# Slot attention: read weights made and read by 64-column tiles instead of 128-column ones

## Chip, cores and metric

One core of one Trainium2 chip runs the whole program. The metric is the device time of one execution in microseconds (us). The kernel before takes 5117.4 us, the median of 3 runs (5113.7 to 5121.28). All data is float32.

## What is computed

The program is a decoder of two layers over 4096 tokens (64 sequences of 64 tokens, 256 wide). The change touches only the first operation of the first layer, a gated slot attention with 16 heads, 128 slots per head and 128-wide keys and values. For each head and token it runs

```
gt = exp(g_t);  bw = beta_t * w_t
Sk = Sk * gt[None, :] + k_t[:, None] * bw[None, :]      # keys x slots
Sv = Sv * gt[:, None] + bw[:, None] * v_t[None, :]      # slots x values
a  = softmax(q_t @ Sk * SCALE)                          # over the slots
o_t = a @ Sv
```

and then normalizes `o_t`, gates it with a sigmoid, projects it with Wo and adds it to X. The recurrence restarts with each sequence of 64 tokens.

## The kernel before

The function `gsa` has no step-by-step scan. A token t reads what an earlier token s has written, weighed by the product of the gates between them. That product is built by levels: at level b (1, 2, 4, 8, 16, 32) it links a block of b tokens with its partner block of b tokens. So the read weights (source s by reader t) are a diagonal (s = t) and six levels, each of which is right only inside its own blocks.

The work is cut in pairs: `pair(h, gp)` runs 4 times for each head h, 64 times in all, and a pair has two halves, named a and b by the ends of the tile names, with 4 tiles of 128 tokens each (a tile is two sequences). The halves are the same code half a pair apart, on PSUM banks 0 to 3 (a) and 4 to 7 (b). In one call of `pair` three generations are in flight: `within` (new, n), `before` (m = n - 1) and `earlier` (l = n - 2). Each engine has its own list of these steps, written out by hand, and the lists meet only at semaphores. Each engine runs its list strictly in order, so a wait holds all that stands behind it.

Names of half a (half b is alike, its lines are in brackets):

- `GWVa` holds the gates (columns 0 to 511), the write weights w (512 to 1023) and the values v. The levels of decay are multiplied into w in place (`early`, `late`).
- `Pa` (six levels of packed left factors) and `AMa` (six levels of packed right factors) feed the level matmuls. DVE makes `AMa` in six products from `AAa`, the softmax weights, and the gates (L1527 to L1540, signal `reach_a_by_dve`).
- PE makes each level with two 128x128 matmuls (L1222, L1230, L1238, L1243, L1247, L1254; signal `weights_a_by_pe`), interleaved with other PE work and before the projection L1260.
- The diagonal is the row sum of `WTa * CAa` (four tensor_tensor_reduce on DVE, L1517), which POOL spreads over `QKa[:, 512:1024]` (L1895).
- DVE lays the levels over it with six predicated copies (L1534, L1539, L1544, L1549, L1553, L1559; signal `weights_a_by_dve`), each between other DVE work.
- PE reads: four 128x128 matmuls of the values with these weights (L1265, signal `read_a_by_pe`), before the projection L1269.
- ACT waits for that read before it writes new write weights and values over `GWVa` (L1779, `Silu`, and L1784), squares the result for the norm (L1782), and evicts the next projection to `CWV` (L1791). DVE runs the convolution on that (L1588, L1602, L1617).
- PE's projection L1260 writes PSUM bank 6. Until then bank 6 holds the output gate, which ACT evicts in L1765 (`SGb`, signal `sigmoid_b_by_act`). PE waits for that before L1260.
- A half begins for ACT with the exponentials of its softmax (L1740 for a, L1656 for b), which wait for the scaled maximum of DVE (L1499, L1365).

The wait of ACT, unchanged by the diff:

```python
if before:
    act.wait_ge(read_a_by_pe, m * 2 + 1)
nc.scalar.activation(forward(GWVa[:, 512:1536]), forward(CWV[:, :]), ACT.Silu).then_inc(silu_a_by_act, 1)
```

Of the kernel before, what the change touches and what calls it, by code (L numbers as in the profile page):

```python
# [6 lines left out]
I32 = mybir.dt.int32  # L7
# [771 lines left out]
def gsa(nc, io, X, PS, IDENT, FLIP, shared, blank):  # L779
    ctx = ExitStack()  # L780
    with ctx:
# [16 lines left out]
        MASKS = sb("masks", [128, 7, 256])  # L798
# [5 lines left out]
        GWVa, GWVb = sb("gwva", [128, 1536]), sb("gwvb", [128, 1536])  # L804
# [7 lines left out]
        Pa, Pb = sb("pa", [128, 6, 256]), sb("pb", [128, 6, 256])  # L812
# [8 lines left out]
        dcola, dcolb = sb("dcola", [128, 4]), sb("dcolb", [128, 4])  # L821
# [200 lines left out]
        with nc.Block() as block:  # L1022

            @block.tensor
            def _(pe):
                pe.wait_ge(setup_by_pool, 1)
                pe.wait_ge(setup_loads_sp, 48)

                def pair(h, gp, within=True, before=True, earlier=True, eldest=True):
# [5 lines left out]
                    if before:  # L1035
                        if earlier:
                            pe.wait_ge(residual_a_by_dve, l * 1 + 1)
                        for e in range(2):
                            last = nc.tensor.transpose(tile(PS[3][:, 0:256], e), tile(Pa[:, 1, :], e), IDENT[:, :])
# [10 lines left out]
                    if before:  # L1050
                        pe.wait_ge(turned_a_by_act, m * 6 + 2)
                        for j in range(4):
                            last = nc.tensor.transpose(tile(PS[3], j), tile(GWVa[:, 1024:1536], j), IDENT[:, :])
# [8 lines left out]
                    if earlier:  # L1062
                        pe.wait_ge(reach_b_by_dve, l * 6 + 1)
                        for e in range(2):
                            last = nc.tensor.matmul(tile(PS[6][:, 0:256], e), tile(Pb[:, 0, :], e), tile(AMb[:, 0, :], e), start=True, stop=True)
                        last.then_inc(weights_b_by_pe, 1)
# [5 lines left out]
                    if earlier:  # L1072
                        pe.wait_ge(reach_b_by_dve, l * 6 + 3)
                        for e in range(2):
                            last = nc.tensor.matmul(tile(PS[4][:, 0:256], e), tile(Pb[:, 1, :], e), tile(AMb[:, 1, :], e), start=True, stop=True)
                        last.then_inc(weights_b_by_pe, 1)
                    if before:
                        pe.wait_ge(values_a_by_act, m * 1 + 1)
                        for e in range(2):
                            last = nc.tensor.transpose(tile(PS[3][:, 0:256], e), tile(Pa[:, 3, :], e), IDENT[:, :])  # L1080
                        last.then_inc(turned_a_by_pe, 1)
                    if earlier:
                        pe.wait_ge(weights_b_by_dve, l * 6 + 1)
                        for e in range(2):
                            last = nc.tensor.matmul(tile(PS[6][:, 0:256], e), tile(Pb[:, 2, :], e), tile(AMb[:, 2, :], e), start=True, stop=True)
                        last.then_inc(weights_b_by_pe, 1)
                        if before:
                            pe.wait_ge(sigmoid_b_by_act, m * 2 + 1)
                        for e in range(2):
                            last = nc.tensor.matmul(tile(PS[7][:, 0:256], e), tile(Pb[:, 4, :], e), tile(AMb[:, 4, :], e), start=True, stop=True)  # L1090
                        last.then_inc(weights_b_by_pe, 1)
                        pe.wait_ge(weights_b_by_dve, l * 6 + 2)
                        for e in range(2):
                            last = nc.tensor.matmul(tile(PS[4][:, 0:256], e), tile(Pb[:, 3, :], e), tile(AMb[:, 3, :], e), start=True, stop=True)
                        last.then_inc(weights_b_by_pe, 1)
# [3355 lines left out]
```

## Time and profile before

| | |
|---|---|
| median of 3 runs | 5117.4 us |
| profiled execution | 5121.28 us among the runs; its span 5121.6 us |
| PE busy | 4927.6 us, 96% of the span |
| DVE busy | 4230.1 us, 83% |
| ACT busy | 3733.4 us, 73% |
| POOL busy | 2307.0 us, 45% |

### The profile page before, as it was taken

How to read it: one execution, taken by the hardware profiler on the slowest of the kernel's cores; microseconds unless marked ns; L12 is line 12 of the kernel's file. 1: busy time of each engine (PE TensorE's matmuls, PEld its weight loads, DVE VectorE, ACT ScalarE, POOL GpSimd, SP SyncE). 2: the span in 40 equal slices, each digit the busy share in tenths (PEclk: the TensorE clock that was granted, in tenths of full speed). 3: DMA queues.
4: the chain of work that ended last, by engine and by line, in shares of the span. 5: the costliest groups of instructions: out<-in, count | busy, mean ns of one | idle time of the engine just before them, and what ended most of it. 6: DMA issues, size and time to landing. Idle time of an engine off the chain costs nothing. (4 is left out here: it accounts for less than half of the span.)

```text
span 5121.6 us, 113480 instructions
## 1 busy us (share of the span) xinstructions
PE 4927.6 (96%) x37926; PEld 3636.5 (71%) x37926; DVE 4230.1 (83%) x10048; ACT 3733.4 (73%) x9700; POOL 2307.0 (45%) x2976
## 2 busy tenths in 40 slices
PE   7999999999999999999999997979999989989899
PEld 4777777777777777777777776868756667778666
DVE  4999999999999999999999995869722378868423
ACT  4999999999999999999999995748713444446233
POOL 2555555555556565655555553741133200011332
PEclk9999999999999999999999998989999999999999
DMA  5500000000000000000000001010012471010225
GB/s 170 173 3 8 6 3 8 7 2 8 7 3 7 7 4 6 8 6 3 8 6 3 8 1 33 17 35 2 24 73 90 135 248 61 2 47 22 87 96 164
DMA packets 178268, 204.34 MB, mean 40 GB/s; under 512 B 28683, under 2 KB 165772, under 8 KB 177040
## 3 DMA queue, kind: packets, MB, share of 16 engines
q1 hardware_dynamic: 161840, 159.07, 10.2%
q0 software_dynamic: 12960, 34.63, 1.8%
q8 instruction: 332, 5.44, 0.4%
q10 hardware_dynamic: 2880, 3.10, 0.2%
q14 instruction: 256, 2.10, 0.1%
HBM read 157.95 MB, written 114.16 MB: 53 GB/s over the span
## 5 line engine op out<-in xcount | busy, mean ns | idle before, releaser
L471 ACT ACTIVATE sl<-PSA 128x512 f32<-128x512 f32 x58 | 34.6, 597 | 253.6 <-PE PSA L172 249.0
L1900 POOL TENSOR_TENSOR gsa_qkb<-gsa_qkb,gsa_tmpb 128x256 f32<-128x256 f32 x64 | 47.7, 745 | 316.3 <-DVE gsa_tmpb L1555 316.3
L1863 POOL TENSOR_TENSOR gsa_qka<-gsa_qka,gsa_tmpa 128x256 f32<-128x256 f32 x64 | 47.6, 744 | 312.1 <-DVE gsa_tmpa L1422 312.1
L274 DVE TENSOR_TENSOR hidden<-sl,PSA 128x512 f32<-128x512 f32 x60 | 41.2, 686 | 173.9 <-ACT sl L471 164.8
L1857 POOL TENSOR_TENSOR gsa_qkb<-IDENT,gsa_dcolb 128x512 f32<-128x512 f32 x64 | 66.5, 1039 | 187.4 <-DVE gsa_dcolb L1379 187.4
L1895 POOL TENSOR_TENSOR gsa_qka<-IDENT,gsa_dcola 128x512 f32<-128x512 f32 x64 | 66.5, 1040 | 184.3 <-DVE gsa_dcola L1517 184.3
L1111 PE MATMUL PSA<-XT,gsa_wa 128*128 128x512 f32 x256 | 123.2, 604 | 9.8 <-DMA gsa_wa<-in_w_heads 7.9
L415 DVE COPY ffn0b_hT<-PSA 128x256 f32<-128x256 f32 x71 | 30.2, 425 | 122.8 <-PE PSA L213 121.1
L415 DVE COPY ffn1b_hT<-PSA 128x256 f32<-128x256 f32 x71 | 30.1, 425 | 121.3 <-PE PSA L213 119.6
L548 POOL DMA_INDIRECT results<-ffn1b_Y,ffn1b_XI x71 | 69.8, 983 | 119.6 <-ACT ffn1b_Y L494 115.6
L548 POOL DMA_INDIRECT results<-ffn0b_Y,ffn0b_XI x71 | 69.5, 979 | 118.6 <-ACT ffn0b_Y L494 113.0
L1157 PE MATMUL PSA<-gsa_wo,gsa_sgb 128*128 128x256 f32 x512 | 122.7, 383 | 0.0
L1323 PE MATMUL PSA<-XT,gsa_wa 128*128 128x512 f32 x256 | 121.7, 598 | 0.0
L1122 PE MATMUL PSA<-XT,gsa_wa 128*128 128x512 f32 x256 | 121.6, 598 | 0.0
L3005 POOL TENSOR_TENSOR ffn0a_rstd<-ffn0a_mse,ffn0a_exponent 128x1 f32<-128x1 f32 x32 | 17.6, 551 | 230.7 <-DVE ffn0a_mse L2814 230.7
L1305 PE MATMUL PSA<-gsa_wo,gsa_sga 128*128 128x256 f32 x512 | 121.1, 379 | 0.0
L1178 PE MATMUL PSA<-XT,gsa_wa 128*128 128x512 f32 x256 | 121.0, 595 | 0.0
L1260 PE MATMUL PSA<-XT,gsa_wa 128*128 128x512 f32 x256 | 120.5, 593 | 0.0
L1191 PE MATMUL PSA<-XT,gsa_wa 128*128 128x512 f32 x256 | 120.5, 593 | 0.0
L1334 PE MATMUL PSA<-XT,gsa_wa 128*128 128x512 f32 x256 | 120.5, 593 | 0.0
L1269 PE MATMUL PSA<-XT,gsa_wa 128*128 128x512 f32 x256 | 120.4, 593 | 0.0
L2415 POOL TENSOR_TENSOR mlstm_rs<-mlstm_wide,mlstm_neghalf 128x16 f32<-128x16 f32 x32 | 96.0, 3000 | 45.1 <-DVE mlstm_wide L2277 44.9
(853 smaller groups left out, 19369.6 us busy)
## 6 DMA issues: line engine op xcount, KB each, us to landing
pairs<-in_blank SPq DMA_DIRECT2D x2, 35904.0 KB, 128.9
ffn0b_XS<-pairs SPq DMA_DIRECT2D x71, 132.0 KB
ffn1b_XS<-pairs SPq DMA_DIRECT2D x71, 132.0 KB
gsa_wa<-in_w_heads SPq DMA_DIRECT2D x64, 128.0 KB, 2.1
X<-in_x SPq DMA_DIRECT2D x8, 512.0 KB, 8.0
mlstm_CX<-in_ctx SPq DMA_DIRECT2D x32, 128.0 KB, 2.1
ffn0b_WGU<-results SPq DMA_DIRECT2D x8, 512.0 KB, 5.2
ffn0b_WD<-results SPq DMA_DIRECT2D x8, 512.0 KB, 6.0
```

The costliest lines, as they stand in the source:

```text
L548: nc.gpsimd.indirect_dma_start(RESULTS[:, :], bass.IndirectOffsetOnAxis(ap=XI[t % IS][:, :], axis=0), Y[t % YS][:, :], None, bounds_check= ...
L1111: last = nc.tensor.matmul(PS[2][:, :], WA[:, 3, c, :], XT[:, c, gp * 1024 + 0:gp * 1024 + 0 + 512], start=(c == 0), stop=(c == 1))
L1122: last = nc.tensor.matmul(PS[3][:, :], WA[:, 2, c, :], XT[:, c, gp * 1024 + 0:gp * 1024 + 0 + 512], start=(c == 0), stop=(c == 1))
L1157: last = nc.tensor.matmul(PS[6 + j // 2][:, (j % 2) * 256:(j % 2) * 256 + 256], tile(SGb[:, :], j), WO[:, :], start=True, stop=True)
L1178: last = nc.tensor.matmul(PS[0][:, :], WA[:, 1, c, :], XT[:, c, gp * 1024 + 0:gp * 1024 + 0 + 512], start=(c == 0), stop=(c == 1))
L1191: last = nc.tensor.matmul(PS[1][:, :], WA[:, 0, c, :], XT[:, c, gp * 1024 + 0:gp * 1024 + 0 + 512], start=(c == 0), stop=(c == 1))
L1260: last = nc.tensor.matmul(PS[6][:, :], WA[:, 3, c, :], XT[:, c, gp * 1024 + 512:gp * 1024 + 512 + 512], start=(c == 0), stop=(c == 1))
L1269: last = nc.tensor.matmul(PS[7][:, :], WA[:, 2, c, :], XT[:, c, gp * 1024 + 512:gp * 1024 + 512 + 512], start=(c == 0), stop=(c == 1))
L1305: last = nc.tensor.matmul(PS[2 + j // 2][:, (j % 2) * 256:(j % 2) * 256 + 256], tile(SGa[:, :], j), WO[:, :], start=True, stop=True)
L1323: last = nc.tensor.matmul(PS[4][:, :], WA[:, 1, c, :], XT[:, c, gp * 1024 + 512:gp * 1024 + 512 + 512], start=(c == 0), stop=(c == 1))
L1334: last = nc.tensor.matmul(PS[5][:, :], WA[:, 0, c, :], XT[:, c, gp * 1024 + 512:gp * 1024 + 512 + 512], start=(c == 0), stop=(c == 1))
L2415: nc.gpsimd.tensor_tensor(rs[b][:, :], wide[b][:, :], NEGHALF[:, :], ALU.pow).then_inc(rs_by_pool, 1)
```

## The change

`GWVa` grows to 2048 columns, so that the raw write weights survive beside the decayed ones. The read weights of a tile are kept as 64 columns for each of its two sequences: sequence r lies on partitions 64r to 64r + 63. All levels, and the diagonal too (raw write weights times `AAa`), come from matmuls with 64 stationary columns (a column tile) and 64 or 32 moving columns, in one burst. DVE then multiplies the diagonal by a mask and lays six levels over it, one behind the other. The read is eight matmuls on 64 rows each (row tiles) and its result lies in two banks. The sums on DVE and the spreading on POOL for the diagonal go. A new mask array of 512 KB is loaded at the start of `gsa`; the old one shrinks from 896 to 768 KB.

On PE, for half a (b is alike, on banks 4, 6 and 6, 7). The six levels of two matmuls each, L1222 to L1254, stood before the projection L1260, with waits for DVE between them. The burst stands right behind L1260, and the read behind L1269, L1275 and L1279 (a projection and slots of half b), right ahead of the transposes L1285:

```diff
-  pe.wait_ge(reach_a_by_dve, m * 6 + 1)
-  for e in range(2):
-      last = nc.tensor.matmul(tile(PS[2][:, 0:256], e), tile(Pa[:, 0, :], e), tile(AMa[:, 0, :], e), ...)
-  last.then_inc(weights_a_by_pe, 1)
...
   if within:
       if before:
           pe.wait_ge(sigmoid_b_by_act, m * 2 + 2)
       for c in range(2):
           last = nc.tensor.matmul(PS[6][:, :], WA[:, 3, c, :], XT[:, c, ...], ...)
   if before:
-      pe.wait_ge(weights_a_by_dve, m * 6 + 6)
-      for j in range(4):
-          last = nc.tensor.matmul(tile(PS[2], j), tile(GWVa[:, 1024:1536], j), tile(QKa[:, 512:1024], j), ...)
-      last.then_inc(read_a_by_pe, 1)
+      pe.wait_ge(reach_a_by_dve, m * 6 + 6)
+      for j in range(4):
+          for r in range(2):
+              nc.tensor.matmul(PS[0][64*r:64*r+64, j*64:j*64+64], part(GWVa[:, 1024:1536], 2*j+r), part(flat(AAa), 2*j+r), ...)
+      for j in range(4):
+          for r in range(2):
+              nc.tensor.matmul(PS[2][64*r:64*r+64, j*32:j*32+32], part(GWVa[:, 1024:1536], 2*j+r), step_rights(AMa[:, 0, :], j, r), ...)
+      for k, bank, at0 in ((1, 0, 256), (2, 2, 128), (3, 0, 384), (4, 2, 256), (5, 2, 384)):
+          for e in range(2):
+              for r in range(2):
+                  last = nc.tensor.matmul(PS[bank][64*r:64*r+64, at0+e*64:at0+e*64+64], part(Pa[:, k-1, :], 2*e+r), part(AMa[:, k, :], 2*e+r), ...)
+      last.then_inc(weights_a_by_pe, 1)
...
+  if before:
+      pe.wait_ge(weights_a_by_dve, m * 7 + 7)
+      if within:
+          pe.wait_ge(sigmoid_a_by_act, n * 2 + 1)
+      for j in range(4):
+          for r in range(2):
+              last = nc.tensor.matmul(PS[2 + r][:, j*64:j*64+64], tile(GWVa[:, 1536:2048], j)[64*r:64*r+64, :], part(QKa[64*r:64*r+64, 512:768], j), ...)
+      last.then_inc(read_a_by_pe, 1)
```

On DVE, for half a. The six products of `AMa` stay, now without copies between them. The six copies of 128x256 (L1534, L1539, L1544, L1549, L1553, L1559) become a product and six copies of 128x128, behind L1564, L1568 and L1569 and ahead of L1572 and L1575. Those for 4, 8, 16 and 32 look like the one for 2 and wait each for the one before:

```diff
-  for j in range(4):
-      last = nc.vector.tensor_tensor_reduce(tile(WTa[:, :], j), tile(CAa[:, :], j), ..., dcola[:, j:j + 1])
-  last.then_inc(diagonal_a_by_dve, 1)
...
-  nc.vector.copy_predicated(rights(QKa[:, 512:1024], 4), packs(MASKS[:, 2, :].bitcast(I32), 4), packs(PS[2][:, 0:256], 4)).then_inc(weights_a_by_dve, 1)
...
+  dve.wait_ge(weights_a_by_pe, m + 1)
+  nc.vector.tensor_tensor(QKa[:, 512:768], PS[0][:, 0:256], WMASKS[:, 0:256], ALU.mult).then_inc(weights_a_by_dve, 1)
+  dve.wait_ge(weights_a_by_dve, m * 7 + 1)
+  dve.sem_inc(passed_by_dve, 1)
+  nc.vector.copy_predicated(square_step_rights(QKa[:, 512:768]), WMASKS[:, 256:384]..., PS[2][:, 0:128]...).then_inc(weights_a_by_dve, 1)
+  dve.wait_ge(weights_a_by_dve, m * 7 + 2)
+  dve.sem_inc(passed_by_dve, 1)
+  nc.vector.copy_predicated(square_rights(QKa[:, 512:768], 2), packs(level_mask(1), 2), packs(PS[0][:, 256:384], 2)).then_inc(weights_a_by_dve, 1)
...
-  nc.vector.scalar_tensor_tensor(SGa[:, :], SGa[:, :], NW[:, 0:1], PS[2][:, :], ALU.mult, ALU.mult)
+  for r in range(2):
+      last = nc.vector.scalar_tensor_tensor(of_part(SGa[:, :], r), of_part(SGa[:, :], r), NW[:, 0:1], PS[2 + r][:, 0:256]..., ALU.mult, ALU.mult)
```

On ACT, the copy of the step-1 left factors (L1793) becomes one of the odd raw write weights into the decayed ones, of the same size, and the square L1782 reads two banks. On POOL, L1895 goes, and the product of the softmax sums (L1901) waits for `softmax_a_by_act`. On SP:

```diff
   nc.sync.dma_start(MASKS[:, :, :], io["masks"]).then_inc(setup_loads_sp, 16)
+  nc.sync.dma_start(WMASKS[:, :], io["weight_masks"]).then_inc(setup_loads_sp, 16)
```

## Rows read from the trace of the kernel before

**Rows 1.** The page, part 1: busy us (share of the span) xinstructions.

```profile
PE 4927.6 (96%) x37926; PEld 3636.5 (71%) x37926; DVE 4230.1 (83%) x10048; ACT 3733.4 (73%) x9700; POOL 2307.0 (45%) x2976
```

**Rows 2.** Busy time by stretch: stretch, length, busy us of PE, PEld, DVE, ACT, POOL, clock.

```profile
1000.00:1500.00 500.00, 497.67 (x2786) 362.14 (x2785) 497.44 (x1176) 459.90 (x1223) 293.40 (x388) 1.00 0.02 5
...
3098.00:3109.00 11.00, 7.49 (x29) 5.46 (x29) 3.53 (x9) 1.09 (x2) 1.02 (x1) 0.83 0.00 0
```

**Rows 3.** Timeline of ACT in one half: start us, length us, engine, line, what, [idle before].

```profile
1010.52 0.37 ACT L1740 ACTIVATE gsa_caa<-PSA,gsa_nmxa 128x128 f32<-128x128 f32 x1 [0.31 <-DVE gsa_nmxa L1499]
...
1017.52 0.68 ACT L1765 ACTIVATE gsa_sgb<-PSA,gsa_bg 128x512 f32<-128x512 f32 x1
...
1019.51 0.42 ACT L1772 ACTIVATE gsa_pb<-gsa_gwvb 128x256 f32<-128x256 f32 x1 [0.73 <-DVE gsa_gwvb L1550]
...
1020.52 1.28 ACT L1779 ACT_TABLE_LOAD   x1
1021.86 0.63 ACT L1779 ACTIVATE gsa_gwva<-gsa_cwv 128x512 f32<-128x512 f32 x1
...
1023.70 1.10 ACT L1791 ACTIVATE gsa_cwv<-PSA,gsa_wcv 128x1024 f32<-128x1024 f32 x1
...
1033.81 0.37 ACT L1656 ACTIVATE gsa_cab<-PSA,gsa_nmxb 128x128 f32<-128x128 f32 x1 [0.30 <-DVE gsa_nmxb L1365]
```

**Rows 4.** Timeline of PE in the same half.

```profile
1014.96 0.61 PE L1222 MATMUL PSA<-gsa_ama,gsa_pa 128*128 128x128 f32 x4
...
1017.94 0.61 PE L1247 MATMUL PSA<-gsa_ama,gsa_pa 128*128 128x128 f32 x4
1018.38 0.38 PE L1250 MATMUL PSA<-IDENT,gsa_pb 128*128 128x128 f32 x2
...
1019.05 1.88 PE L1260 MATMUL PSA<-XT,gsa_wa 128*128 128x512 f32 x4
1020.77 1.05 PE L1265 MATMUL PSA<-gsa_qka,gsa_gwva 128*128 128x128 f32 x8
1021.66 1.88 PE L1269 MATMUL PSA<-XT,gsa_wa 128*128 128x512 f32 x4
```

**Rows 5.** Timeline of DVE in the same half.

```profile
1018.72 0.45 DVE L1549 COPY_PREDICATED gsa_qka<-gsa_masks,PSA 128x256 f32<-128x256 int32 x1
...
1020.06 0.43 DVE L1559 COPY_PREDICATED gsa_qka<-gsa_masks,PSA 128x256 f32<-128x256 int32 x1
...
1025.21 1.26 DVE L1588 SCALAR_TENSOR_TENSOR gsa_cwv<-PSA,gsa_wcv,gsa_cwv 128x1008 f32<-128x1008 f32 x1
...
1033.11 0.66 DVE L1365 TENSOR_SCALAR gsa_nmxb<-gsa_mxb 128x4 f32<-128x4 f32 x1
```

**Rows 6.** Groups of instructions from 1000 to 1500 us: busy us, mean ns, idle.

```profile
L1517 DVE CUSTOM_DVE_ANT_0 gsa_wta<-gsa_caa,gsa_wta 128x128 f32<-128x128 f32 x44 | 10.0, 279 | 0.0
...
L1534 DVE COPY_PREDICATED gsa_qka<-gsa_masks,PSA 128x256 f32<-128x256 int32 x11 | 7.9, 721 | 0.0
...
L1539 DVE COPY_PREDICATED gsa_qka<-gsa_masks,PSA 128x256 f32<-128x256 int32 x11 | 7.9, 714 | 0.0
...
L1544 DVE COPY_PREDICATED gsa_qka<-gsa_masks,PSA 128x256 f32<-128x256 int32 x11 | 4.7, 430 | 0.0
...
L1555 DVE TENSOR_TENSOR gsa_tmpb<-PSA,gsa_gb 128x256 f32<-128x256 f32 x11 | 4.6, 418 | 0.0
```

**Rows 7.** Timeline of PE where it switches to tiles of the array, later stages.

```profile
3210.84 0.38 PE L2131 MATMUL PSA<-IDENT,mlstm_CX 128*128 128x128 f32 x2
3211.15 2.04 PE L2188 MATMUL PSA<-mlstm_V,mlstm_S 64*64 64x17 f32 x64
...
3417.03 1.13 PE L2630 MATMUL PSA<-ffn0a_V,ffn0a_PT 128*64 128x34 f32 x32
3417.98 1.07 PE L2669 MATMUL PSA<-ffn0a_WV,ffn0a_xT 128*64 128x128 f32 x16
```

**Rows 8.** DMA issues from 64 to 75 us: count, KB, median us to landing.

```profile
gsa_masks<-in_masks SPq DMA_DIRECT2D x1, 896.0 KB, 4.8
```

More of the change, by code:

```diff
@@ L1219, in pair @@
                     if before:
-                        pe.wait_ge(reach_a_by_dve, m * 6 + 1)
-                        for e in range(2):
-                            last = nc.tensor.matmul(tile(PS[2][:, 0:256], e), tile(Pa[:, 0, :], e), tile(AMa[:, 0, :], e), start=True, stop=True)
-                        last.then_inc(weights_a_by_pe, 1)
                         pe.wait_ge(level_b_by_dve, m * 6 + 1)
@@ L1244, in pair @@
[L1244 to L1250 removed]
+                            last = nc.tensor.transpose(tile(PS[5][:, 0:256], e), tile(Pb[:, 1, :], e), IDENT[:, :])
@@ L1251, in pair @@
                         last.then_inc(turned_b_by_pe, 1)
-                        pe.wait_ge(weights_a_by_dve, m * 6 + 3)
-                        for e in range(2):
-                            last = nc.tensor.matmul(tile(PS[2][:, 0:256], e), tile(Pa[:, 5, :], e), tile(AMa[:, 5, :], e), start=True, stop=True)
-                        last.then_inc(weights_a_by_pe, 1)
                     if within:
@@ L1280, in pair @@
                         last.then_inc(slots_b_by_pe, 1)
+                    if before:
+                        pe.wait_ge(weights_a_by_dve, m * 7 + 7)
+                        if within:
+                            pe.wait_ge(sigmoid_a_by_act, n * 2 + 1)
+                        for j in range(4):
+                            for r in range(2):
+                                last = nc.tensor.matmul(PS[2 + r][:, j * 64:j * 64 + 64], tile(GWVa[:, 1536:2048], j)[64 * r:64 * r + 64, :], part(QKa[64 * r:64 * r + 64, 512:768], j), start=True, stop=True)
+                        last.then_inc(read_a_by_pe, 1)
                     if within:
@@ L1671, in pair @@
                         for j in range(4):
[L1672 removed]
+                            last = nc.scalar.activation(tile(GWVa[:, 1536:2048], j), tile(PS[3], j), ACT.Copy, scale=c4a[:, j:j + 1])
                         last.then_inc(values_a_by_act, 1)
@@ L4324, in level_masks @@
     out = []
-    for lv in range(6):
+    for lv in range(1, 6):
         b = 2 ** lv
@@ L4331, in level_masks, with weight_masks @@
     return np.stack(out, 1)
+def weight_masks():
+    s, t = np.arange(128)[:, None] % 64, np.arange(64)[None, :]
+    out = [np.tile(s == t, (1, 4))]
+    u = np.arange(32)[None, :]
+    out += [s == 2 * u, s == 2 * u, s == 2 * u + 1, s == 2 * u + 1]
+    for lv in range(1, 6):
+        block = t // 2 ** lv
+        partner = np.where(block % 2 == 1, block - 1, block + 1)
+        out.append(np.tile(s // 2 ** lv == partner, (1, 2)))
+    return np.concatenate(out, 1).astype(np.float32)
 def mirrored(x):
```

320 lines of the change are left out of this document (138 added, 182 removed).

## Prediction, written before the change was run

> **What bounds the kernel now.** I read the page first: PE 96%, DVE 83%, ACT 73% busy [rows 1]. Then the busy time by stretch, because the change lives in the slot attention alone (74 to 3070 us of 5121.6). From 1000 to 1500 us PE is busy 497.7, DVE 497.4 and ACT 459.9 of 500 us [rows 2]: three engines are nearly full, at a granted clock of 1.00. The reader should see that no engine has more than 8% to give, so a wait of some microseconds that hits one of them isn't hidden; it comes out at the end. A pair takes 46.7 us, a half 23.3: ACT starts the softmax of half a at 1010.52 and that of half b at 1033.81 [rows 3]. There are 64 pairs, so 128 halves.
>
> Next I laid the three queues of one half beside each other. ACT goes without a hole from L1740 to the eviction of the output gate, L1765, which ends at 1017.52 + 0.68 = 1018.20. It idles 0.73 us at L1772 and 0.30 us before L1656 [rows 3]. Its wait for the read (L1779) costs nothing today: the read L1265 ends at 1020.77 + 1.05 = 1021.82, and the table load for L1779 ends at 1021.80 [rows 3, 4]. PE starts L1260 at 1019.05 [rows 4], 0.85 us after the gate that it must wait for was evicted, so that wait costs nothing either. These two waits are the ones to watch.
>
> **The change, part by part.** I follow half a; half b has the same order of steps on every engine.
>
> (1) Level matmuls. Removed: 12 matmuls, 24 records. The four of one level take 1018.38 - 1017.94 = 0.44 us from the start to the next start [rows 4] (0.61 is the length with the modelled end, which overlaps the next), so 2.66 us. Added: 8 + 8 + 20 = 36 matmuls, 72 records, on 64 stationary columns. Tiles that lie side by side run at once: 32 records with 34 moving columns take 3417.98 - 3417.03 = 0.95 us, 0.029 each; with 128 moving columns 16 records take 1.07 us, of which the last alone is 0.27, so 0.054 each [rows 7]. Ours move 64 or 32 columns. I take 0.029 (for a pair 0.058, and half of the 0.109 for 128 columns is 0.055): 72 x 0.029 = 2.09 us. The upper bound is 72 x 0.054 = 3.9 us. Switching PE to tiles costs about 0.1 us: two transposes from 3210.84 would be through at 3211.06, the tiles start at 3211.15 [rows 7]. PE itself gains some 0.5 us by the levels and loses 0.4 by four switches. So PE's own work hardly changes.
>
> (2) Where the burst stands. Before, the levels filled PE from 1014.96 on [rows 4], while ACT worked towards L1765. Now they stand behind L1260, and L1260 waits for L1765. Ahead of it remain L1226, L1234 and L1250, eight records of 0.11 us with nothing late to wait for, so PE is through at about 1015.9 and then idles some 2.4 us. That is an added wait; queued behind it are L1260, the burst, L1269, L1275, L1279 and the read. So L1260 starts at 1018.20 + 0.15 = 1018.35, lasts 1.72 to the next start [rows 4], then 0.1 + 2.09: the burst's last start is over at 1022.26 and its last record lands at about 1022.43. The six products of DVE that it needs are ready at about 1017 and don't matter.
>
> (3) The evacuation. DVE's copies were spread among other work; now a product and six copies stand in a row, each waiting for the one before. Product of 128x256 from PSUM: 0.42 us by L1555. Copies of 128x256 take 430 ns at block 4 and 721 and 714 ns at blocks 1 and 2 [rows 6]. Those of 128x128 aren't in the trace; the slope between the two forms isn't either. Halving the elements and keeping some 0.16 us fixed gives 0.30 for four of them and 0.44 for the first two (bounds 0.22 to 0.43, and 0.30 to 0.72). The gap between dependent ones: a copy that waited for PE started 1018.72, when the matmuls L1247 had ended at 1018.55 [rows 4, 5], 0.17 us later; dependent DVE instructions without a wait instruction of their own show some 0.03. I take 0.13, near the first, since each copy here has such a wait. Sum: 0.42 + 2 x 0.44 + 4 x 0.30 + 6 x 0.13 = 3.28 us (2.4 to 3.9). It starts about 1022.48 and ends about 1025.76. PE meanwhile does L1269 (1.72) and L1275, L1279 (0.89) and is through at 1024.9.
>
> The Trainium skill, "TensorEngine Tiling (Array Packing)", section Performance Considerations (PSUM Bottleneck), says that tiling speeds up TensorE but not the evacuation of PSUM. That speaks against this change, and the rows above agree with it: 2.09 us on PE are followed by 3.28 us on DVE. Were the evacuation sped up like the matmuls, the sum below would be some 200 us smaller.
>
> (4) The read. L1559 ended at 1020.49 and L1265 started at 1020.77 [rows 4, 5], a lag of 0.28. So the read starts at 1026.04. Its 16 records have 128 stationary columns on 64 rows. No row shows that form with both row tiles in use. If the two run at once, as the 64x64 tiles do (64 records in 2.04 us [rows 7]), they last as long as the eight of L1265, 1.05 us; if not, 1.9. I take 1.05: the read ends at 1027.09 and ACT starts L1779 at 1027.13.
>
> (5) What it sets. L1779 started at 1021.86 [rows 3]: 5.27 us later. ACT had finished its table load at about 1021, since the wait at L1772 (0.73) is gone, so it now stands idle some 6 us in each half. Behind it on ACT are L1782, L1784, L1791 and all to the next softmax; the 0.30 us before L1656 are slack, so 4.97 remain. By DVE it is nearly the same: L1791 ends 2.94 after L1779 begins, at 1030.07; L1588 needs it and moves from 1025.21 to 1030.10, and from there DVE had no hole up to L1365, whose end at 1033.77 [rows 5] becomes 1038.66. Two chains end within 0.1 us of each other, so neither alone could be shortened for a gain. Half: 23.3 + 4.96 = 28.25 us.
>
> (6) What is saved elsewhere is hidden behind this. Four reductions (279 ns each [rows 6]), POOL's spreading, and some 0.6 us of copies come off engines that now wait; the split of L1579 adds about 0.12 us on DVE beside ACT. I count these at nothing: they lie between L1740 and the burst, where the burst waits for ACT. ACT's changed copies have equal sizes: nothing.
>
> (7) Start. SP loads 512 KB more and 128 KB less before the first weights; 896 KB landed in 4.8 us [rows 8]. In proportion 384 KB cost about 2 us once (0 to 5), as all engines wait for it.
>
> **Sum.** 5121.6 + 128 x 4.96 + 2 = 5758 us for the profiled execution, which stands 4 us (0.1%) above the median. So 5754, and I say 5755.
>
> **The rivals.**
> Faster. The place is DVE: if ACT and PE could run the chain of (2) to (4) beside other work, DVE's full queue would be the bound, and it loses per half about 0.85 us of reductions and 0.6 of copies, and gains 0.12: 1.3 us, 128 x 1.3 = 170, giving 4950 us. For it speaks that DVE is at 497.4 of 500 [rows 2]. Against it: ACT would have to be able to start L1779 no later than today, while the chain behind L1765 is 0.15 + 1.72 + 0.1 + 2.09 + 3.28 + 1.05 and lags, 8.9 us, and ACT has 2.8 us of work to put beside it. It decides as soon as that chain is shorter than about 3.7 us. 5%.
> Tiles that don't overlap. If the burst goes at 0.054 and the read's row tiles take turns, +1.8 and +0.85 per half: 5755 + 128 x 2.65 = 6095 us. Against it: both forms of tile ran in pairs in later stages [rows 7]. 7%.
> The clock falls. PE would have holes of 2.4, 1.1 and 1.6 us in each half. Where it was busy 7.5 of 11 us the granted clock was 0.83, here 1.00 [rows 2]. At 0.83 the 4.9 us of PE on the chain (1.72 + 2.19 + 1.05) become 5.9: 5755 + 128 x 1.0 = 5885 us. Wholly at the lower of the clock's two levels, 1.2 instead of 2.4 GHz, they would double: 6380. 12%, mostly near 5885. The Trainium skill, "TensorE: Matmul & The Clock Gate", Part 1, says that the throttled state is the default and activity lifts it, which points the same way; whether these holes suffice no row here shows.
> Partly absorbed. Copies and gaps at their lower bounds (2.4 instead of 3.28) and 0.2 less in the lags: +3.9 per half, 5620 us. 8%.
> That it doesn't do what it says (copies of half the size that cost as much as before): +0.13 x 4 + 0.28 x 2 = 1.1 us in each half: 5895 us. 6%.
>
> **How the numbers follow.** The forecast, 5755 us, has 62%, its own range 5660 to 5850. The range that should hold 8 in 10 takes in the absorbed case, the copies and the mild clock case: 5600 to 5990. It leaves out the faster case, the tiles in turn and the deep clock case. About 0.2% is what a measurement of this kernel can tell from no change. All cases but the first rival are slower by far more than that: slower 0.94, within it 0.01, faster 0.05.
>
> **What would show it.** In the profile after: a half of about 28 us; ACT idle about 6 us before L1779's counterpart (and L1691's), released by the read on PE; PE idle about 2.4 us before the projection of L1260, released by ACT's output gate; DVE's seven instructions in a row over 3.3 us; the level burst in 2.1 us with two records per 0.058 us. ACT's busy share from 1000 to 1500 us, 92% now [rows 2], should be near 76%. If ACT shows no wait for the read, or DVE's copies are short and overlap, I am wrong. If PE's clock is below 1.00 in the slot attention, the clock rival holds.

## The result and the profile after

The changed kernel takes 6054.87 us (median of 4 runs, 6047.3 to 6068.79), the kernel before beside it 5118.67 us (5113.7 to 5121.28): 936 us more, a ratio of 1.184 with a 95% interval of 1.183 to 1.186. The profiled execution has a span of 6045.5 us against 5121.6. The forecast was 5755 (+637), its range ended at 5990.

The page of the kernel after, part 1, answers to [rows 1]:

```profile
PE 5254.6 (87%) x45094; PEld 3839.7 (64%) x45094; DVE 4208.9 (70%) x9280; ACT 3713.3 (61%) x9700; POOL 2194.6 (36%) x2848
```

No engine is nearly full any more. Busy time by stretch of the kernel after (stretch, length, busy us of PE, PEld, DVE, ACT, POOL, granted clock), with the stretch of [rows 2] first and four pieces of single halves behind it:

```profile
1000.00:1500.00 500.00, 420.78 (x3015) 302.80 (x3016) 376.76 (x801) 348.24 (x933) 207.90 (x276) 0.89 0.02 5
1050.40:1052.90 2.50, 0.29 (x3) 0.05 (x1) 1.90 (x6) 2.40 (x6) 0.53 (x1) 1.00 0.04 13
1052.90:1060.00 7.10, 7.04 (x88) 4.58 (x88) 4.06 (x9) 2.73 (x5) 3.21 (x6) 1.00 0.01 2
1022.10:1025.60 3.50, 3.46 (x4) 1.18 (x4) 2.03 (x3) 2.72 (x5) 3.20 (x6) 0.54 0.02 5
1036.60:1039.50 2.90, 2.90 (x10) 2.38 (x9) 2.90 (x8) 2.90 (x11) 2.22 (x4) 0.59 0.00 0
```

The clock is 0.89 where it was 1.00 [rows 2], and it isn't spread evenly: near 1.00 in most pieces, and at 0.5, its lower level of 1.2 GHz, in stretches of some 3 to 7 us, each of which begins in one of PE's holes or within 1.3 us behind it (one goes from 1062.85 to 1069.68, behind the three holes of the half below).

The timeline of PE in one half a (start us, length us, engine, line, what, [idle before]) answers to [rows 4]. L1248 is the projection L1260 of before, L1254 to L1261 are the burst, L1283 is the read:

```profile
1050.31 0.38 PE L1242 MATMUL PSA<-IDENT,gsa_pb 128*128 128x128 f32 x2
1052.94 1.98 PE L1248 MATMUL PSA<-XT,gsa_wa 128*128 128x512 f32 x4 [2.25 <-ACT gsa_sgb L1751]
1054.86 0.69 PE L1254 MATMUL PSA<-gsa_aaa,gsa_gwva 128*64 128x64 f32 x16
1055.37 0.61 PE L1257 MATMUL PSA<-gsa_ama,gsa_gwva 128*64 128x32 f32 x16
1055.81 1.36 PE L1261 MATMUL PSA<-gsa_ama,gsa_pa 128*64 128x64 f32 x40
1057.10 1.98 PE L1265 MATMUL PSA<-XT,gsa_wa 128*128 128x512 f32 x4
...
1060.75 1.11 PE L1283 MATMUL PSA<-gsa_qka,gsa_gwva 64*128 64x64 f32 x16 [0.77 <-DVE gsa_qka L1554]
1063.58 1.12 PE L1289 MATMUL PSA<-IDENT,gsa_gwva 128*128 128x128 f32 x4 [1.73 <-ACT gsa_gwva L1770]
```

The same half on DVE, against [rows 5]: the product and the six copies, with 0.15 us between one's end and the next one's start.

```profile
1057.22 0.42 DVE L1536 TENSOR_TENSOR gsa_qka<-PSA,gsa_wmasks 128x256 f32<-128x256 f32 x1 [1.70 <-PE PSA L1261]
1057.80 0.44 DVE L1539 COPY_PREDICATED gsa_qka<-gsa_wmasks,PSA 128x128 f32<-128x128 int32 x1
...
1058.97 0.30 DVE L1545 COPY_PREDICATED gsa_qka<-gsa_wmasks,PSA 128x128 f32<-128x128 int32 x1 [0.15 <-DVE gsa_qka L1542]
...
1060.31 0.30 DVE L1554 COPY_PREDICATED gsa_qka<-gsa_wmasks,PSA 128x128 f32<-128x128 int32 x1
```

And on ACT, against [rows 3]. The wait that cost nothing before is now 6.25 us:

```profile
1045.21 0.37 ACT L1726 ACTIVATE gsa_caa<-PSA,gsa_nmxa 128x128 f32<-128x128 f32 x1
...
1052.20 0.68 ACT L1751 ACTIVATE gsa_sgb<-PSA,gsa_bg 128x512 f32<-128x512 f32 x1
...
1061.90 0.63 ACT L1765 ACTIVATE gsa_gwva<-gsa_cwv 128x512 f32<-128x512 f32 x1 [6.25 <-PE PSA L1283]
```

From here on a half has two parts: the head, from ACT's first exponential to its Silu, and the tail, from the Silu to the first exponential of the next half. Both are read from ACT's timeline. Means over the pairs between about 500 and 2900 us, in us:

| kernel | head a | tail a | head b | tail b | pair | time less that of before, same chip |
|---|---|---|---|---|---|---|
| before | 11.34 | 11.97 | 11.34 | 12.11 | 46.76 | 0 |
| forecast | 16.61 | 11.64 | 16.61 | 11.64 | 56.50 | +637 |
| after | 17.06 | 13.52 | 17.91 | 12.94 | 61.43 | +936 |

The forecast's head is 1027.13 - 1010.52. In the half shown above it is 1061.90 - 1045.21 = 16.69: there the chain is as forecast, and nothing in it ran at half clock. In others it is up to 18.6. The pattern of heads (16.7, 18.2, 18.6) and tails (12.6, 13.7, 13.9) repeats every four pairs. Where the 299 us beyond the forecast (936 - 637) are stands in the groups of PE's instructions between 1000 and 2000 us (busy us, mean ns of one, idle before). L1309 and L1170 are the output projections of the two halves, L1107 and L1248 the projections behind the output gate, L1126 and L1191 two others of the same form:

```profile
L1309 PE MATMUL PSA<-gsa_wo,gsa_sga 128*128 128x256 f32 x136 | 54.2, 571 | 0.0
L1107 PE MATMUL PSA<-XT,gsa_wa 128*128 128x512 f32 x64 | 50.9, 943 | 36.2 <-ACT gsa_sga L1668 36.2
L1170 PE MATMUL PSA<-gsa_wo,gsa_sgb 128*128 128x256 f32 x128 | 49.0, 553 | 0.0
L1248 PE MATMUL PSA<-XT,gsa_wa 128*128 128x512 f32 x64 | 38.3, 728 | 36.0 <-ACT gsa_sgb L1751 36.0
...
L1126 PE MATMUL PSA<-XT,gsa_wa 128*128 128x512 f32 x64 | 31.7, 618 | 0.0
L1191 PE MATMUL PSA<-XT,gsa_wa 128*128 128x512 f32 x64 | 30.1, 593 | 0.0
```

Projections elsewhere run at the length of before. Of the projections only the two that follow a hole, and the output projections that follow the holes around the read, are slow; so are the small transposes between the read and the output projection (L1299: 438 ns, where e1_filled below has 290).

### The profile page after: what moved, and what is told of

It is laid out like the page before. It is cut to its first block and busy times, and to the rows that moved or that the text cites. A ratio compares the mean times of both kernels' runs of the same rounds, so it can differ in the third digit from the quotient of the medians.

```text
span 6045.5 us, 127114 instructions
## 1 busy us (share of the span) xinstructions
PE 5254.6 (87%) x45094; PEld 3839.7 (64%) x45094; DVE 4208.9 (70%) x9280; ACT 3713.3 (61%) x9700; POOL 2194.6 (36%) x2848
## 3 DMA queue, kind: packets, MB, share of 16 engines
q14 instruction: 255, 2.09, 0.1%
## 5 line engine op out<-in xcount | busy, mean ns | idle before, releaser
L1107 PE MATMUL PSA<-XT,gsa_wa 128*128 128x512 f32 x256 | 204.5, 946 | 150.8 <-ACT gsa_sga L1668 142.1
L1248 PE MATMUL PSA<-XT,gsa_wa 128*128 128x512 f32 x256 | 156.1, 741 | 141.6 <-ACT gsa_sgb L1751 141.6
L1856 POOL TENSOR_TENSOR gsa_qka<-gsa_qka,gsa_tmpa 128x256 f32<-128x256 f32 x64 | 46.5, 727 | 598.4 <-DVE gsa_tmpa L1440 598.4
L1890 POOL TENSOR_TENSOR gsa_qkb<-gsa_qkb,gsa_tmpb 128x256 f32<-128x256 f32 x64 | 46.6, 727 | 552.0 <-DVE gsa_tmpb L1568 552.0
L1107 PEld LDWEIGHTS PSA<-XT,gsa_wa 128*128 128x128 f32 x256 | 67.1, 289 | 223.3 <-ACT gsa_sga L1668 157.0
L1309 PE MATMUL PSA<-gsa_wo,gsa_sga 128*128 128x256 f32 x512 | 204.8, 573 | 0.0
L1170 PE MATMUL PSA<-gsa_wo,gsa_sgb 128*128 128x256 f32 x512 | 197.7, 557 | 0.0
L1309 PEld LDWEIGHTS PSA<-gsa_wo,gsa_sga 128*128 128x128 f32 x512 | 158.6, 325 | 33.4
L1248 PEld LDWEIGHTS PSA<-XT,gsa_wa 128*128 128x128 f32 x256 | 52.2, 226 | 197.8 <-ACT gsa_sgb L1751 156.6
L1170 PEld LDWEIGHTS PSA<-gsa_wo,gsa_sgb 128*128 128x128 f32 x512 | 153.4, 315 | 31.0
L1804 ACT ACTIVATE gsa_caa<-PSA,gsa_c4a 128x128 f32<-128x128 f32 x256 | 73.0, 368 | 126.1 <-PE PSA L1322 126.1
L1879 POOL TENSOR_TENSOR gsa_qkb<-gsa_qkb,gsa_tmpb 128x256 f32<-128x256 f32 x64 | 66.6, 1041 | 206.2 <-DVE gsa_tmpb L1513 206.2
L1843 POOL TENSOR_TENSOR gsa_qka<-gsa_qka,gsa_tmpa 128x256 f32<-128x256 f32 x64 | 66.7, 1042 | 202.9 <-DVE gsa_tmpa L1385 202.9
L1713 ACT ACTIVATE gsa_cab<-PSA,gsa_c4b 128x128 f32<-128x128 f32 x256 | 73.0, 368 | 109.2 <-PE PSA L1183 109.2
L1126 PE MATMUL PSA<-XT,gsa_wa 128*128 128x512 f32 x256 | 129.0, 627 | 0.0
```

What stands on the lines that cost most here:

```text
L1107: last = nc.tensor.matmul(PS[2][:, :], WA[:, 3, c, :], XT[:, c, gp * 1024 + 0:gp * 1024 + 0 + 512], start=(c == 0), stop=(c == 1))
L1126: last = nc.tensor.matmul(PS[3][:, :], WA[:, 2, c, :], XT[:, c, gp * 1024 + 0:gp * 1024 + 0 + 512], start=(c == 0), stop=(c == 1))
L1170: last = nc.tensor.matmul(PS[6 + j // 2][:, (j % 2) * 256:(j % 2) * 256 + 256], tile(SGb[:, :], j), WO[:, :], start=True, stop=True)
L1248: last = nc.tensor.matmul(PS[6][:, :], WA[:, 3, c, :], XT[:, c, gp * 1024 + 512:gp * 1024 + 512 + 512], start=(c == 0), stop=(c == 1))
L1309: last = nc.tensor.matmul(PS[2 + j // 2][:, (j % 2) * 256:(j % 2) * 256 + 256], tile(SGa[:, :], j), WO[:, :], start=True, stop=True)
L1713: last = nc.scalar.activation(tile(CAb[:, :], j), tile(PS[4], j), ACT.Copy, scale=c4b[:, j:j + 1])
```

## The experiments

The theory after the result: the chain of the forecast is right, one to one, and the three holes of PE in each half (2.25, 0.77 and 1.73 us above) make the clock fall just behind them, on work that is on the path. The rivals: the tail is longer for a reason of DVE or ACT; the tiles or the small copies cost it; or the order of the steps has nothing to do with it. Times below are given as the difference from the kernel before, run on the same chip (5095 to 5120 us), since chips differ by some 0.5%.

### All three holes filled: e1_filled

```diff
+ pe.wait_ge(reach_a_by_dve, m * 6 + 1)
+ for _ in range(10): nc.tensor.matmul(PS[2][:, 0:128], IDENT[:, :], IDENT[:, :], ...)     # ahead of the projection
...
+ for _ in range(5): nc.tensor.matmul(PS[3][:, 256:384], IDENT[:, :], IDENT[:, :], ...)    # ahead of the read
...
+ for _ in range(8): nc.tensor.matmul(PS[0][:, 256:384], IDENT[:, :], IDENT[:, :], ...)    # behind the read
```

> The changed kernel, with matmuls of IDENT by IDENT put into PE's three holes of each half: 10 ahead of the projection that waits for the output gate, 5 ahead of the read, 8 ahead of the transposes that wait for the Silu (0.22 us each, into banks that nobody uses at that time; their results are not used). Nothing of the chain is taken away. Theory (my chain of waits is right at full clock; what I missed is the clock, 0.89 in the slot attention, whose slow stretches hit PE work on the chain): the granted clock goes to 1.00, the head of a half (exponentials to Silu) to 16.6 us from 17.1 (a) and 17.9 (b), the tail to 11.7 to 12.0 from 13.2 on average, the time to 5750 to 5800 us. Rival (the tail is longer for reasons of DVE or ACT, not the clock): clock 1.00 and the tails still near 12.6 to 13.8, 5950 us or more. Rival (the clock doesn't follow PE's holes): clock stays near 0.9, time 6050 or more.

5769.85 us against 5098.52, +671. More work on PE made the kernel 265 us faster. The window of [rows 2] and PE's groups from 1000 to 2000 us (L1111 and L1261 are the projections behind the gate, L1328 and L1180 the output projections):

```profile
1000.00:1500.00 500.00, 497.86 (x4025) 377.57 (x4024) 402.45 (x861) 375.18 (x1011) 224.51 (x299) 1.00 0.02 5
```

```profile
L1111 PE MATMUL PSA<-XT,gsa_wa 128*128 128x512 f32 x72 | 35.7, 618 | 0.7
...
L1328 PE MATMUL PSA<-gsa_wo,gsa_sga 128*128 128x256 f32 x144 | 34.1, 379 | 0.0
...
L1261 PE MATMUL PSA<-XT,gsa_wa 128*128 128x512 f32 x68 | 33.7, 618 | 0.4
...
L1180 PE MATMUL PSA<-gsa_wo,gsa_sgb 128*128 128x256 f32 x136 | 32.2, 379 | 0.0
```

The clock is back at 1.00, both kinds of projection have their full speed. Heads are 16.98, tails 11.56 and 11.69 us, where the forecast had 16.61 and 11.64. Of the 0.37 in the head, 0.29 (16.98 - 16.69) is the filling itself, which ends a little late: the read starts 0.41 us behind DVE's row, not 0.14. Over 128 halves that is 37 us, and with the 265 it makes up the 299 beyond the forecast. The tails of the changed kernel were longer by the clock alone; the rival of DVE or ACT is out.

### One hole filled at a time: e5_hole1, e6_hole3

Each is one third of the edit above.

> The changed kernel with only the first hole of each half filled: 10 small matmuls ahead of the projection that waits for ACT's output gate; the holes ahead of the read and behind it stay. In the changed kernel two pieces of PE work run at half clock: this projection (946 and 741 ns a record instead of 618) and the output projection behind the read. Theory (each slow stretch belongs to the hole or holes right ahead of it): the projection goes to 618 ns, the output projection stays slow, tails near 13.2, 5930 to 5990 us. Rival (the chip reacts to all idle time of PE together, so that one hole less frees both): tails near 11.7, 5780 to 5830 us. Rival (it makes no difference which is filled because the first hole isn't what matters): 6040 or more.

> The changed kernel with only the third hole of each half filled: 8 small matmuls behind the read, ahead of the transposes that wait for the Silu. Theory (each slow stretch belongs to the hole right ahead of it): the output projection (571 and 553 ns a record) goes to 379, tails from 13.2 to 11.7, so 1.5 us less in each half, 5850 us; the projection behind the first hole stays slow, heads 17.1 to 17.9. Rival (all idle together): everything at full clock, 5760 to 5800 us. Rival (the third hole isn't what slows the output projection): 6040 or more.

The same groups, first of e5_hole1, then of e6_hole3 (projections behind the gate in L1255 and in L1250, L1107; output projections in L1316, L1174 and in L1313):

```profile
L1316 PE MATMUL PSA<-gsa_wo,gsa_sga 128*128 128x256 f32 x136 | 58.1, 607 | 0.0
L1174 PE MATMUL PSA<-gsa_wo,gsa_sgb 128*128 128x256 f32 x128 | 54.2, 604 | 0.0
...
L1255 PE MATMUL PSA<-XT,gsa_wa 128*128 128x512 f32 x64 | 31.7, 618 | 0.3
```

```profile
L1250 PE MATMUL PSA<-XT,gsa_wa 128*128 128x512 f32 x68 | 41.4, 740 | 38.3 <-ACT gsa_sgb L1755 38.3
L1107 PE MATMUL PSA<-XT,gsa_wa 128*128 128x512 f32 x68 | 39.7, 712 | 38.5 <-ACT gsa_sga L1672 38.5
...
L1313 PE MATMUL PSA<-gsa_wo,gsa_sga 128*128 128x256 f32 x136 | 32.2, 379 | 0.0
```

With the first hole filled: heads 16.69 and 16.72, but tails 14.01 and 14.03, 6033.75 us or +933, outside the 5930 to 5990 that I expected. With the third filled: tails 11.57 and 11.70, heads 17.78 and 17.41, 5852.55 us or +751. So where PE is slow does follow from the holes right ahead of it, but the holes don't act each for itself. What I did not expect is that e5_hole1 gained nothing: the heads became 1.56 us a pair shorter and the tails 1.58 longer, since now every output projection ran slow and not only some (607 ns against 571). By the profile's record of the clock, PE is at the lower level for 553 us between 500 and 3000 us in both kernels, with the first hole filled always from the hole behind the read on; with the third filled it is 164 us. The gains don't add up: 3 us for the first hole, 185 for the third, 265 for all three. The second hole was not filled alone.

### The burst ahead of the projection: e2_ahead

```diff
+ # burst (unchanged), with its wait for reach_a_by_dve
  pe.wait_ge(sigmoid_b_by_act, m * 2 + 2)
  # projection into PS[6]
- # burst
```

> The changed kernel with one edit: the burst of level matmuls stands ahead of the projection that waits for the output gate, not behind it; DVE's order and the read stay. Theory (serial chain behind ACT's gate): the burst starts when the sixth product of DVE is there, 6.1 us after the exponentials, not 10.0; the copies now wait for DVE's own earlier work until 10.4 and end at about 13.8, so the Silu comes at about 15.0 instead of 17.1 and 17.9: 1.6 to 2.5 us less in each half, 5730 to 5850 us. Rival (tiles or copies cost it, wherever they stand): 6000 to 6055.

5711.64 us, +613: 323 less than the changed kernel for moving one block. By time that is 18 us below the range that I gave. Heads are 14.91 and 14.94, as expected. Tails are 13.01 and 13.27, the clock from 1000 to 1500 us is 0.90: the holes around the read are still there. The rival that tiles or copies cost the same wherever they stand is out.

### The placement without the tiles: e4_wide

From the kernel before: its twelve 128-column level matmuls behind the projection, the six copies in one row, the read behind the slots.

```diff
  # projection into PS[6]
+ pe.wait_ge(reach_a_by_dve, m * 6 + 6)
...
+ for k, bank, at0 in ((0, 2, 0), (1, 0, 0), (2, 2, 256), (3, 0, 256), (4, 3, 0), (5, 3, 256)):
+     for e in range(2):
+         last = nc.tensor.matmul(tile(PS[bank][:, at0:at0 + 256], e), tile(Pa[:, k, :], e), tile(AMa[:, k, :], e), ...)
```

> The kernel before, with its 128-column levels, sums and POOL's spreading untouched, but with the placement of the change: twelve level matmuls in one burst behind the projection, the six 128x256 copies in one row on DVE, and the read behind the second projection and the slots. Theory (the placement alone costs the time, not the 64-column tiles): burst 2.66 us, copies 0.72 + 0.71 + 4 x 0.43 and six gaps of 0.15, 4.1 us, read 1.05: some 0.9 us more in each half than the changed kernel, 6100 to 6200 us. Rival (the tiles cost it): near the kernel before, 5120 to 5300.

6274.04 us, +1175, the slowest of all. PE's timeline in one half b (L1082 is the projection, L1090 the levels, L1111 the read):

```profile
1207.03 3.09 PE L1082 MATMUL PSA<-XT,gsa_wa 128*128 128x512 f32 x4 [2.26 <-ACT gsa_sga L1636]
1209.91 3.46 PE L1090 MATMUL PSA<-gsa_amb,gsa_pb 128*128 128x128 f32 x24
...
1217.55 1.16 PE L1111 MATMUL PSA<-gsa_qkb,gsa_gwvb 128*128 128x128 f32 x8 [1.57 <-DVE gsa_qkb L1391]
```

The placement alone, with the matmuls and copies of before, loses everything that the change lost and more. In this placement the tiles and small copies make it better by 239 us, not worse: the burst of tiles takes 2.24 us, these levels 3.29 (at full clock 2.66 by [rows 4]). My 6100 to 6200 was too low by 74 us at its upper end, for the reason the forecast was: the clock is 0.88 from 1000 to 1500 us, and the levels are now part of what runs slowly behind the hole.

### The row on DVE shorter and longer: e3_fewcopies, e11_longer

e3_fewcopies leaves out the copies of levels 4 to 32 (`weights_a_by_dve` counts 3 instead of 7 a half). e11_longer is e1_filled with the last copy done five times and 11 instead of 5 fillers ahead of the read.

> The changed kernel without the predicated copies of levels 4, 8, 16 and 32 (left out of the computation; all matmuls stay). Theory (DVE's row of seven is on the path that sets the end, one to one): 4 copies of 0.30 us and their gaps of 0.15, 1.8 us less in each half, 230 us: 5815 us, or up to 80 less if the clock rises with the smaller hole. Rival (the copies are hidden beside the projection on PE, which is what the read really waits for): at most 0.5 us a half, 5990 or more.

> As e1_filled (clock held at 1.00), with the last copy of DVE's row done five times instead of once, each waiting for the one before, and six more small matmuls in the hole ahead of the read. Theory (the row on DVE is on the path one to one once the clock is held): 4 x (0.30 + 0.15) = 1.8 us more on DVE, less 0.35 us by which the filling held the read back in e1_filled, 1.45 us in each half, 185 us: 5955 us. Rival (part of the row is covered by PE's second projection or by ACT): less than 1.0 us, under 5900. Rival (more work on DVE also delays its later work): over 2.0 us, above 6020.

e3_fewcopies: 5770.93 us, +672, so 264 less, inside what I wrote, but not for the reason I wrote. In the halves at full clock the head shrank from 16.69 to 15.87 us only, 0.82 and not 1.8: PE then has no wait for DVE before the read, its own queue (burst, second projection, slots) is what the read waits for. The rest came from the clock, 0.97 against 0.89 from 1000 to 1500 us, since the hole ahead of the read was gone. The sum agreed by two errors that cancel. e11_longer, with the clock held, is the clean one: 5966.87 us against 5095.38, +871 where e1_filled had +671, heads 18.45 and 18.54 instead of 16.98, tails unchanged at 11.58 and 11.70. That is 1.5 us for the 1.45 expected: one more microsecond on DVE's row costs one microsecond a half as soon as it is longer than PE's queue beside it. A shorter row pays only for the first 0.82 us.

### Can the tiles pay? e7_split, e8_late_first, e9_tmp, e10_early

e7_split keeps the tiles and undoes the serial chain: the burst ahead of the projection and in two parts by bank, DVE's row right behind the products with two decays in it, the read right behind the projection.

```diff
+ pe.wait_ge(reach_a_by_dve, m * 6 + 3)
+ # diagonal, levels 2 and 8 -> PS[0];  weights_a_by_pe + 1
+ pe.wait_ge(reach_a_by_dve, m * 6 + 6)
+ # levels 1, 4, 16, 32 -> PS[2];  weights_a_by_pe + 1
  # projection into PS[6]
+ pe.wait_ge(weights_a_by_dve, m * 7 + 7)
+ # read
```

> The changed kernel with the chain moved back to where it can run beside other work: the burst ahead of the projection and in two parts by bank (diagonal, levels 2 and 8 into one bank, levels 1, 4, 16 and 32 into the other), the first part waiting for three of DVE's products only; DVE's seven instructions right behind the six products, with the two decays of block 8 between them; the read right behind the projection. Theory (what costs the time is the serial chain behind the output gate, and the clock that falls with it; the tiles themselves are cheap): copies end about 9.6 to 10.0 us after the exponentials, the read about 11.2, ACT is ready for the Silu at about 11.3 as in the kernel before, clock 0.98 or more, and DVE has 1.3 us less work in each half: 5000 to 5120 us. Rival (64-column tiles, or the small copies, cost of themselves): 5200 to 5600.

5129.57 us against 5101.08, ratio 1.0062 (1.0046 to 1.0079). 908 of the 936 us are back; the range that I had given, 5000 to 5120, is missed by 10. Heads are 11.39 and 11.31 us, the clock from 1000 to 1500 us is 1.00:

```profile
1000.00:1500.00 500.00, 489.28 (x3944) 346.68 (x3942) 467.35 (x1043) 457.46 (x1208) 270.62 (x364) 1.00 0.02 5
```

But it is not faster than the kernel before. DVE has 467 us of work in 500, against 497 [rows 2], and the saved 1.3 us a half are idle time. What ACT, DVE and PE wait for in this kernel, 1000 to 2000 us (waiting line <- releasing line: us in total, times, longest):

```profile
ACT gsa_gwva L1781 <- PE PSA L1281: 19.8, 21, 1.0
...
DVE gsa_qka L1537 <- PE PSA L1258: 11.3, 21, 0.5
...
PE PSA L1281 <- DVE gsa_qka L1558: 10.9, 21, 0.5
```

DVE's row waits 0.5 us for the first part of the burst, the read waits 0.5 us for the row, ACT's Silu 1.0 us for the read. I tried three small changes on this.

> As e7_split, with one decay of block 8 moved ahead of DVE's product, where DVE waits 0.54 us for the first part of the burst, and the other right behind the product. Theory (DVE's queue is the bound again, and the wait of ACT for the read, 1.0 us a half, follows it): 0.4 us less in each half, 5060 to 5090 us, faster than the kernel before by 0.2 to 0.8%. Rival (ACT or PE bounds it and DVE's wait is free): 5125 to 5135.

> As e8_late_first, with one more product (the level of the other half) between two dependent copies of DVE, where 0.15 us pass unused. Theory (DVE's queue is the bound): 0.1 us less in each half than e8_late_first, 10 to 20 us. Rival (the read, which comes 0.25 us later, is the bound): 20 to 40 us more than e8_late_first.

> As e7_split, with the first part of the burst earlier on PE: the diagonal as soon as the first product is there, levels 2 and 8 behind one slot matmul group, both ahead of four transposes. In e7_split and e8_late_first DVE had its six products at 1186.19 but PE ended the first part at 1186.6, and seven dependent instructions, the read and the Silu of ACT hang on that. Theory (this chain, not DVE's queue, sets the half): 0.45 us less in each half less 0.1 to 0.2 for two more switches of the tile size, 5075 to 5105 us where the kernel before has 5114, about the same or up to 0.8% faster. Rival (DVE's queue or PE is the bound): 5130 to 5160.

None beat the kernel before, and the times expected for e8_late_first (5060 to 5090) and e10_early (5075 to 5105) are missed by 56 and 71 us. e8_late_first: 5146.46 against 5113.96, 1.0065, the same as e7_split: the decay now fills DVE's wait, but the product still starts when PE is done, and nothing behind it moves. e9_tmp: 5178.94, 1.0128. Its heads are those of e8_late_first (11.40 and 11.33) and its tails 0.22 and 0.25 us longer; in it ACT waits 0.4 us a half for a decay of DVE further down (L1723 for L1476), which stands behind the moved product; no run separates the two. e10_early: 5176.29 against 5120.15, 1.0114: its heads are 11.69 and 11.58, 0.3 longer. By the timelines PE lost more by two more changes of the tile than the earlier start gained. PE's timeline in one half of e8_late_first and of e10_early, from slots (128*128) to tiles (128*64) and back:

```profile
1184.57 0.61 PE L1090 MATMUL PSA<-gsa_ama,gsa_lta 128*128 128x128 f32 x4
1185.01 0.38 PE L1095 MATMUL PSA<-IDENT,gsa_pa 128*128 128x128 f32 x2
...
1185.54 0.69 PE L1105 MATMUL PSA<-gsa_aab,gsa_gwvb 128*64 128x64 f32 x16
1186.06 0.64 PE L1109 MATMUL PSA<-gsa_amb,gsa_pb 128*64 128x64 f32 x16
1186.52 0.61 PE L1114 MATMUL PSA<-gsa_amb,gsa_gwvb 128*64 128x32 f32 x16
```

```profile
1197.42 0.69 PE L1091 MATMUL PSA<-gsa_aab,gsa_gwvb 128*64 128x64 f32 x16
1198.04 0.71 PE L1095 MATMUL PSA<-gsa_ama,gsa_lta 128*128 128x128 f32 x4
1198.68 0.69 PE L1102 MATMUL PSA<-gsa_amb,gsa_pb 128*64 128x64 f32 x16
1199.29 0.44 PE L1107 MATMUL PSA<-IDENT,gsa_pa 128*128 128x128 f32 x2
```

The four slot records take 0.44 us from start to start among others of their kind, 0.64 between two tile bursts (1198.68 - 1198.04); the diagonal 0.62 instead of 0.52, the levels 0.61 instead of 0.46. The Trainium skill, "TensorEngine Tiling (Array Packing)", section Key Properties, says that a change of the tiling mode drains TensorE. The trace shows a loss at such places that fits this, 0.1 to 0.2 us for each.

Why e7_split ends 0.6% behind isn't settled. Its heads equal those of before; its tails are 12.14 and 12.17 against 11.97 and 12.11. That is 0.24 us a pair, 16 us over the 64 pairs; in the traces another 8 us lie behind the last Silu of half a, where the last halves run out. Which wait makes that difference no run here isolates.

## Why the prediction was right and wrong

The direction and the chain of waits were right. The step that failed is the clock: the sum had no term for it, and the rival that had one priced it at 1.0 us a half, where 2.46 were measured. So the size was 299 us short, and the range missed by 65.

- (1) Burst 2.09 us, forecast from rows of other stages [rows 7]: 1057.10 - 1054.86 = 2.24. Right. A switch at 0.1: the projection ahead took 1.92 to the next start instead of 1.72, so 0.2. Slightly low.
- (2) PE idle 2.4 us ahead of the projection, released by ACT's gate: 2.25 by L1751. Right. Start 0.15 after the gate: 0.06.
- (3) DVE's row 3.28 us: 1060.61 - 1057.22 = 3.39, with copies of 0.44 and 0.30 us as taken, and gaps of 0.15 for 0.13. Right; the rival of copies that cost as much as the full-sized ones is out.
- (4) Lag 0.28 and read 1.05: 0.14 and 1.11. Right: the records of the read start in pairs, 0.01 us apart, and one pair follows the other by 0.112 us, so the two row tiles do run side by side. The rival of tiles in turn is out.
- (5) Silu 5.27 us later in the half: 5.35 (16.69 - 11.34) at full clock. e11_longer shows the slope. That both chains behind it absorb nothing but 0.30: right, e1_filled has the tails forecast.
- (6) Savings elsewhere count nothing: right in the changed kernel, and even in e7_split, where DVE has them as idle time.
- (7) Start +2 us: no run separates it. The new masks landed in 5.4 us by the table of DMA issues.
- ACT's share 76%: it was 348.24 of 500, 70%, because the halves were longer still.

What failed is how the clock was put in: as a rival with 12% and not as a term, and, more, at what price. I had written down the holes myself, 2.4, 1.1 and 1.6 us, and the row with clock 0.83 at a share of 7.5 in 11 us [rows 2]; PE's share here came out as 421 in 500, and the clock as 0.89. Yet I left it out of the forecast, as if it were an alternative to the chain. It is a consequence of the chain: with the chain as it is and only its holes filled, the clock is 1.00 (e1_filled). The price had two faults. First, I spread a mean clock, 0.83, evenly over the PE work in the head (1.72 + 2.19 + 1.05, which is 4.96 and not 4.9), 1.0 us a half. The slow stretches aren't spread: they start in a hole or behind it, and what stands behind a hole is, in this chain, the work that others wait for. Spread evenly, the measured mean of 0.89 would cost 4.96 / 0.89 - 4.96 = 0.6 us; measured are 0.45 (a) and 1.30 (b) in the heads. Second, the tail's PE work wasn't in the price at all, since ACT and DVE set the tail. The output projection took 1039.50 - 1036.61 = 2.89 us to the next start in the piece from 1036.60 above (clock 0.59), where the eight records of half a took 1027.72 - 1025.99 = 1.73 in the kernel before, and ACT, which waited 0.54 us there before, waits 2.17 in the half after 1061.90. These are the rows, first of the kernel after, then of the kernel before:

```profile
1036.61 3.06 PE L1170 MATMUL PSA<-gsa_wo,gsa_sgb 128*128 128x256 f32 x8
1039.50 0.61 PE L1176 MATMUL PSA<-gsa_ama,gsa_lta 128*128 128x128 f32 x4
...
1072.09 1.14 ACT L1804 ACTIVATE gsa_caa<-PSA,gsa_c4a 128x128 f32<-128x128 f32 x4 [2.17 <-PE PSA L1322]
```

```profile
1025.99 1.89 PE L1305 MATMUL PSA<-gsa_wo,gsa_sga 128*128 128x256 f32 x8
1027.72 0.61 PE L1310 MATMUL PSA<-gsa_amb,gsa_ltb 128*128 128x128 f32 x4
...
1029.86 1.14 ACT L1818 ACTIVATE gsa_caa<-PSA,gsa_c4a 128x128 f32<-128x128 f32 x4 [0.54 <-PE PSA L1318]
```

Against the forecast, tails grew by 1.88 and 1.30. Together with the heads that is 4.93 us a pair, 2.46 a half where I had 1.0.

The Trainium skill, "TensorE: Matmul & The Clock Gate", section "HAM oscillation — how this bites in real kernels", describes a loop in which TensorE waits once an iteration and is throttled anew each time. The slow stretches here come back in the same way, once or twice in a half, but behind three short holes and not one long wait. Had I read it for what repeats and not only for whether it can happen, I would have added chain and clock: 5885 even at my low price (5755 + 128 x 1.02), and 5755 + 128 x 2.46 = 6070 at the measured one.

The other rival that ended on the faster side needed a chain behind the gate below 3.7 us. It is 9.0 (from 1052.88 to 1061.90), so it never came near; e7_split, where nothing of the chain is behind the gate but the read, shows that even then the saved DVE work is not worth time.

## What to carry to other kernels

When a change makes an engine wait in a kernel whose TensorE was full, price the wait and the clock together, and put the slow stretch on the work right behind each hole, also where another engine sets the pace there. A hole filled alone may only move the slow stretch to the next one; test all of them at once. Tiles that make matmuls cheap don't help if they turn interleaved steps into one burst, one row of copies and one read. Where the steps stand decided 908 of the 936 us here. What they are made of decided less: 239 us in favour of the tiles in the serial placement, nothing gained in the interleaved one.

## What the runs showed of the hardware, not expected

- Three holes of 2.25, 0.77 and 1.73 us in a half of 30.7 us brought the granted clock to 0.89 on average, with stretches of some 3 to 7 us at the lower level; with the holes filled it was 1.00. With the first hole filled alone it stayed at 0.88.
- Adding 23 small matmuls to each half made the kernel 265 us faster.
- A change between 128x128 and 128x64 tiles cost 0.1 to 0.2 us on the work around it.
- In DVE's row of seven, each instruction waits for the one before and starts 0.15 us after its end; independent ones of the same kernel start some 0.08 us before that end (0.41 us long, 0.33 from start to start). Over the six gaps of the row that is 1.4 us.
